# Causal attention: the mask of the diagonal blocks is added by VectorE instead of by a product with the identity

## The reference

```
h = _layernorm(x, ln_w, ln_b)
h = conv over time, 3 taps, one filter for each channel
q, k, v = split(h @ attn_w)            # 16 heads of 8 channels, rotary positions on q and k
scores = q @ k^T / sqrt(8)
scores = where(causal, scores, -1e30)
y = softmax(scores) @ v
x = x + y @ proj_w
```

## Time and profile before

| what | value |
|---|---|
| median of 3 runs | 1771.7 us (1768.62 to 1781.09) |
| profiled execution | 1771.55 us, span of its records 1769.7 us |
| TensorE busy, all of the span | 1417.7 us (80%) |
| VectorE busy | 1041.1 us (59%) |
| ScalarE busy | 704.1 us (40%) |
| GpSimd busy | 572.9 us (32%) |
| L998, reductions of the rounds of L0f | 88, 97.2 us in all |
| L904, mask products of L0f | 176, one pair a round |
| first and last reduction of L998 | 293.3 and 468.0 us from the start |

### The profile page before, as it was taken

The page is one execution under the profiler, slowest core; times in us unless marked ns, Lnnn a source line. Parts: engine busy times, 40 slices in busy tenths (PEclk is TensorE's granted clock), DMA queues, the critical chain, the costliest instruction groups (busy, mean ns, idle before and its releaser), DMA issues. The chain is left out here.

```text
span 1769.7 us, 23757 instructions
## 1 busy us (share of the span) xinstructions
PE 1417.7 (80%) x8978; PEld 724.7 (41%) x8980; DVE 1041.1 (59%) x1468; ACT 704.1 (40%) x1306; POOL 572.9 (32%) x594
## 2 busy tenths in 40 slices
PE   5868755788858999699668986699999657689984
PEld 3345522333333444344234434354554232256553
DVE  3698736677642222578366752466676145468866
ACT  2444431666720000277334753244444221255522
POOL 1477713453302110332113301634422100047660
PEclk7789986899969999889886996899999669879986
DMA  3000010000010000100010002000000000000000
GB/s 102 0 1 0 1 44 1 1 1 1 1 75 0 0 0 0 50 1 1 9 49 1 1 1 44 1 1 1 2 2 1 1 29 0 6 1 1 2 1 26
DMA packets 19154, 20.58 MB, mean 12 GB/s; under 512 B 9803, under 2 KB 15163, under 8 KB 18408
## 3 DMA queue, kind: packets, MB, share of 16 engines
q1 hardware_dynamic: 18024, 19.07, 3.5%
q10 hardware_dynamic: 1024, 0.07, 0.0%
HBM read 17.94 MB, written 1.05 MB: 11 GB/s over the span
## 5 line engine op out<-in xcount | busy, mean ns | idle before, releaser
L1663 ACT ACTIVATE L2f_prob<-P 128x512 f32<-128x512 f32 x160 | 86.8, 595 | 112.6 <-PE P L1601 112.6
L998 DVE TENSOR_REDUCE L0f_nm<-P 128x2 f32<-128x768 f32 (+3 forms) x88 | 97.2, 1121 | 42.7 <-PE P L904 42.5
L2174 PE MATMUL P<-L0m_hm,L0m_w 128*128 128x512 f32 x256 | 112.5, 600 | 2.6 <-POOL L0m_hm L2136 2.6
L1691 DVE TENSOR_REDUCE L2f_nm<-P 128x2 f32<-128x768 f32 (+3 forms) x88 | 99.2, 1128 | 3.0
L1601 PE MATMUL P<-L2f_qs,L2f_ks 49*128 49x384 f32 (+3 forms) x512 | 94.3, 477 | 7.7 <-ACT L2f_prob L1663 3.9
L954 ACT ACTIVATE L0f_prob<-P 128x512 f32<-128x512 f32 x160 | 87.3, 601 | 29.4 <-PE P L917 26.9
L1517 POOL TENSOR_SCALAR_AFFINE_SELECT L2f_prob<-L2f_prob 128x512 f32<-128x512 f32 x64 | 39.7, 635 | 168.1 <-ACT L2f_prob L1663 168.0
L1690 DVE TENSOR_TENSOR P<-P,L2f_mask 128x256 f32<-128x256 f32 (+2 forms) x88 | 48.4, 550 | 74.3 <-PE P L1587 73.1
L1587 PE MATMUL P<-L2f_ks,L2f_qs 48*128 48x384 f32 (+3 forms) x512 | 87.7, 451 | 3.4 <-DVE L2f_nm L1691 3.4
L2516 POOL TENSOR_TENSOR L3x_exm<-L3x_exm,L3x_rec 128x2048 f32<-128x2048 f32 x16 | 72.3, 4526 | 26.1 <-DVE L3x_rec L2690 26.1
L2174 PEld LDWEIGHTS P<-L0m_hm,L0m_w 128*128 128x128 f32 x256 | 49.2, 193 | 64.9 <-issue 62.8
(11 more groups left out here) (575 smaller groups left out, 3298.7 us busy)
## 6 DMA issues: line engine op xcount, KB each, us to landing
L0m_w<-in_L0m_w SPq DMA_DIRECT2D x1, 2048.0 KB, 7.7
L0f_va<-in_L0f_va SPq DMA_DIRECT2D x3, 512.0 KB, 4.7
in_xt<-in_x SPq DMA_DIRECT2D x1, 1024.0 KB
L0x_segi<-in_segb SPq DMA_DIRECT2D x1, 1024.0 KB, 5.0
L0m_w<-in_L0m_w SPq DMA_DIRECT2D x1, 1024.0 KB, 9.7
out<-out_o SPq DMA_DIRECT2D x4, 256.0 KB, 2.5
L1x_va<-in_va SPq DMA_DIRECT2D x3, 256.0 KB, 3.1
L1x_vr<-in_vr SPq DMA_DIRECT2D x3, 256.0 KB, 4.3
```

The source lines that it names most:

```text
L998: nc.vector.tensor_reduce(S.nm[:, qt, first:first + 2 * many].rearrange("p (i e) -> p e i", e=2), P[:, bank:bank + 2, 0:many * width].rear ...
L1663: nc.scalar.activation(S.group_prob(b, g)[:, slot, :], P[:, bank, :], ACT.Exp).then_inc(*S.act_done.up())
L1691: nc.vector.tensor_reduce(S.nm[:, qt, first:first + 2 * many].rearrange("p (i e) -> p e i", e=2), P[:, bank:bank + 2, 0:many * width].rear ...
L2174: m = mm(P[:, bank, :], lhs, hm[:, e, :], start=e == 0, stop=e == E - 1)
```

## The change

TensorE no longer multiplies the identity with the mask. In each round the products of L901 are now complete by themselves, and the last of them signals s_full. VectorE, when the round is full, adds the mask to the diagonal blocks of both banks in PSUM with one instruction (in place), waits for its end, and reduces as before. The order of the steps is the same.

```diff
                     for p in range(many):
                         for e in range(2):
                             pair = 4 * half + many * i + p
-                            mm(P[:, bank + e, p * width:(p + 1) * width], S.qs1[b % 2][64 * e:64 * e + 48, pair, qt * 128:(qt + 1) * 128],
-                               S.ks[b % 2][64 * e:64 * e + 48, pair, 0:width], start=p == 0, stop=False)
-                    for e in range(2):
-                        m = mm(P[:, bank + e, 0:many * width].rearrange("p (h k) -> p h k", k=width)[:, :, width - 128:width],
-                               G["identb"][:], mask[:].unsqueeze(1).to_broadcast([128, many, 128]), start=False, stop=True)
+                            m = mm(P[:, bank + e, p * width:(p + 1) * width], S.qs1[b % 2][64 * e:64 * e + 48, pair, qt * 128:(qt + 1) * 128],
+                                   S.ks[b % 2][64 * e:64 * e + 48, pair, 0:width], start=True, stop=True)
                     m.then_inc(*S.s_full.up())
...
                     first = 8 * half + 2 * many * i
+                    diag = P[:, bank:bank + 2, 0:many * width].rearrange("p e (i k) -> p e i k", k=width)[:, :, :, width - 128:width]
+                    over = mask[:].unsqueeze(1).unsqueeze(1).to_broadcast([128, 2, many, 128])
+                    link(dve, nc.vector.tensor_tensor(diag, diag, over, ALU.add), S.vstep)
                     nc.vector.tensor_reduce(S.nm[:, qt, first:first + 2 * many].rearrange("p (i e) -> p e i", e=2),
```

## The result

| | before | changed |
|---|---|---|
| median, 6 runs each | 1771.53 us (1768.62 to 1781.09) | 1793.68 us (1791.96 to 1796.29) |
| profiled execution | 1771.55 us, span 1769.7 | 1792.71 us, span 1791.0 |

The changed kernel is slower by 22 us: the ratio is 1.0115, with a 95% interval of 1.0087 to 1.0142.

What follows compares the result with a forecast made beforehand. VectorE was taken to bound the lead and to end each stretch's chain, with no engine full in the stretches. Lead 5.7, stretches 14.5 and clock 3.0 made 23.2 us on 1771.55: 1795 us, range 1784 to 1807.

Steps and rivals of the forecast that it cites:

- What bounds it: Phase L0f: VectorE bounds the lead; in seven stretches no engine is full, each a chain ending through VectorE.
- Price of the additions: VectorE in L0f: each addition costs 1.27, 0.72 or 0.46 us by width, 51.1 us for eight halves.
- Lead, +5.7: L0f's opening, only first-half rounds: VectorE never idle, so additions fully paid, 6.39 less 0.69 us for removed products.
- Stretches, lag 12.5 to 16.0, taken 14.5: L0f's seven steady stretches: added VectorE time carried as a lag that waits shrink, 12.5 to 16.0 us, taken 14.5.
- one of the prediction's own signs of being wrong: Splitting of the maxima before the transposes: forecast wrong if its 1.85 us became shorter or longer.
- Clock, +3.0, two of five blocks turned slow: Transpose blocks after each split: longer TensorE standing turns two of five fast blocks half-speed, 1.5 us each, +3.0.
- After the last maximum nothing moves: L0f's last pass, without rounds, and everything behind it: only the start shifts, no added time.
- Later phases: Phases behind L0f, which the change doesn't touch: counted at nothing.
- The one within 1%: Lead and stretches: VectorE packs its work and head waits close, 13.3 us, 1785; chance 0.15 for within 1%.
- The third, clock and feedback at +33: L0f: all five blocks turn slow and later bank pairs hold up exponentials, 33.2 us, 1805; chance 0.25.

Runs made afterwards that it cites:

- e1: Changed kernel without its 88 additions, so no mask at all in the L0f rounds; 1771.95 us, ratio 1.0012 to the kernel before.
- e2: Kernel before with the 88 VectorE additions put in and TensorE's mask products kept, so the mask is added twice; 1792.81 us, ratio 1.0114.
- e7: Changed kernel with every mask addition made twice; 1830.55 us in one run, 36.9 us over the changed kernel.
- e3: Changed kernel with six unneeded TensorE products ahead of its wait for the split maxima, once a half; 1792.72 us, ratio 1.0117.
- e9: Changed kernel with three unneeded TensorE products ahead of each exponential step of the last pass only; 1800.3 us (2 runs).
- e11: Kernel before with VectorE additions replacing mask products only in the lead's eleven rounds; 1775.91 us, ratio 1.0021.
- e4: Kernel before with six unneeded TensorE products ahead of its wait for the split maxima, once a half; 1771.71 us, ratio 0.9988.
- e10: Kernel before with VectorE additions replacing mask products only in the last two halves' rounds; 1775.06 us, ratio 1.0020.

## Why the prediction was right, point by point

The time was 1793.7 for a forecast of 1795, the sign and the size were right. By its own terms:

**What bounds it** held. TensorE's products were worth nothing (e1 in the total, e2 in the stretches), although TensorE had the highest busy time. VectorE became the bound (157.08 of 172.56 us, e7 97%).

**Price of the additions** held: 1.26, 0.73 and 0.47 us from start to start in the timeline above and its neighbours, against 1.27, 0.72 and 0.46 in L2f. VectorE's busy time in all rose by 41.1 us and not by about 48: the 88 additions by themselves sum to 47.8, but the split of the maxima became 3.8 us shorter over its eight times, and more of VectorE's instructions overlap.

**Lead, +5.7:** measured 5.3 (changed, e2, e3, e9 and e11, all at 26.3). The products that I took off, 0.69, are not in it, and can't be: this length starts with VectorE's first round, behind the first pair of products. Ahead of it VectorE waited 11.15 us before and 10.64 in the changed kernel, so the pair was worth about 0.5. What is in the 5.3 is a shorter split of the maxima, 1.6 us from the start of L418 to the block in place of 2.6.

**Stretches, lag 12.5 to 16.0, taken 14.5:** measured 11.75 (e3 less e4, with some of the clock left in it), below the range of this term. The order by stretch is right in the middle (1.9, 2.5, 1.8, 2.2 for 1.7, 2.6, 1.6, 2.7), and too large in the first, the sixth and the last (-0.3, 0.2, 3.5 for 0.8, 2.1, 4.5). The count took the split as fixed, and its change was one of the prediction's own signs of being wrong. From the start of the split to the block it was 1.8 us before the block at 453.48, and it is 1.15 before that at 469.39:

```profile
469.39 1.38 PE L372 MATMUL P<-identb,L0f_qk 128*128 128x128 bf16 x16 [2.24 <-DVE L0f_qk L421]
```

with L418 starting at 468.24, in the row of the timeline above. The four small instructions ran beside GpSimd's clearing of the exponentials (L867), and where they now begin, it is done. The traces of all kernels bear this out (last section): with no GpSimd instruction beside them the four took 1.09 to 1.11 us in each of 31 splits. In e10, where only the last two stretches changed, only the last two splits became as short.

**Clock, +3.0, two of five blocks turned slow:** measured 3.4 (changed less e3; an estimate, since e3 still has three slow blocks and the filler takes time itself), but by another count: three of the five turned fully slow and the other two in part (1.40 and 1.38 us), and in the mean each cost less than my 1.5.

**After the last maximum nothing moves:** wrong. The last pass took 5.0 us more, by the clock. I had looked for the clock's effect only at the block behind each wait, and the eighth block, the one at the head of the last pass, I priced like the rest. But there TensorE went on at half speed for 17 us. Its short stands between the exponentials don't explain that: they are 0.78 us in the kernel before as well, where the clock held (second line of each pair: before).

```profile
499.98 0.61 PE L914 MATMUL P<-L0f_qs,L0f_ks 51*128 51x384 bf16 x4 [0.78 <-ACT L0f_prob L951]
476.66 0.40 PE L917 MATMUL P<-L0f_qs,L0f_ks 51*128 51x384 bf16 x4 [0.78 <-ACT L0f_prob L954]
503.34 0.61 PE L914 MATMUL P<-L0f_qs,L0f_ks 51*128 51x512 bf16 x2 [0.78 <-ACT L0f_prob L951]
479.01 0.39 PE L917 MATMUL P<-L0f_qs,L0f_ks 51*128 51x512 bf16 x2 [0.78 <-ACT L0f_prob L954]
```

Over all kernels without filler in it the length of this pass ("last" in the table) goes with the clock granted in it: 21.9 us at 0.93, 23.0 at 0.89, 23.2 at 0.87, 23.7 at 0.86, 24.0 at 0.82, 25.7 at 0.77, and 26.8 to 26.9 at 0.69. What sets the clock there stays open. This term was mis-sized from 0 to 5.0.

**Later phases** I left at nothing, and they gave back 4.1 us, for which I find no cause in the change. Without the later phases and the last pass, the terms as measured give nearly the same: 5.3 + 11.75 + 3.4 = 20.45 us, 1792.0. The 5.0 and the 4.1 nearly cancel by chance, so the agreement to 1.3 us is better than the working deserves; on the two profiled executions it is 21.2 us against 23.2.

**Rivals.** The one within 1% priced packed work at 13.3 us, 7.5 of it in the stretches. The head waits did close in part (31.4 to 10.1 us), and the measured lag of 11.75 lies between its 7.5 and my 14.5, just under the 12.0 that I had named as the border; the clock decided against it. The third, clock and feedback at +33, put the clock at 7.5; it was 3.4 in the stretches and 5.0 behind them. Its feedback is not separated by any run: TensorE's waits for the bank pairs did rise (17.1 us of its weight loads, 1.7 before), and ScalarE's waits for the exponentials' products rose from 26.7 to 36.0 us in the seven stretches. A lag below the count leaves little room for it, no more.

## What to carry to other kernels

Price a moved operation by the waits of the engine that gets it, in the order in which they lie, not by its share of busy time: the same kind of instruction cost 3 us in all where waits follow it, and 21 where they don't, of which 16 to 17 in the stretches and the lead. An engine that reads as the busiest may give nothing when it is spared, and it may even lose clock: look also at the stretches that the edit leaves alone, and don't put down what you see there to the edit before the same has shown in a second and third variant. And when total times of edits differ by less than the later phases move by themselves, cut the trace at one recurring point and compare lengths.

## What the runs showed of the hardware that I had not expected

TensorE's clock fell to 0.69 over a whole pass of unchanged instructions after edits ahead of it (21.9 us before, 26.8 in e1 and 26.9 in the changed kernel). Which edits do it follows no rule that I found: in e10 the products of the last two stretches are gone too and it was 0.87, and with all products of the stretches in place it was 0.93, 0.86 and 0.82 (before, e2, e11). TensorE's short stands in this pass were the same 0.78 us at either clock. The Trainium skill (TensorE: Matmul & The Clock Gate, "What's actually happening") says that half speed is the default and that activity releases it; e9 agrees, 0.85 with more work in the same place, at no gain in time, but no run here shows what made the same work hold the clock in one kernel and not in the other.

The four instructions that split the maxima took 1.1 to 3.5 us in one and the same kernel, the changed one. The Trainium skill (SBUF — State Buffer, "Who interferes with whom") says that a VectorE instruction with two SBUF inputs contends with a GpSimd instruction that reads SBUF. The rows fit it: the subtraction L419, whose two inputs lie in SBUF, took 0.21 us in the timeline behind 468 us and 1.17 us at 369.23, where GpSimd was at work on the next sequence's splitting. Over the 104 splits in the 13 traces it took 0.21 or 0.22 us in all 48 with no GpSimd instruction beside it, 0.51 to 0.53 beside the clearing L867 alone (17 times), and 0.28 to 1.18 beside other work of GpSimd (39 times). The casts, with one input, became slower too: L420 took 0.24 or 0.25 us alone and up to 1.23 beside GpSimd.

```profile
369.23 1.17 DVE L419 TENSOR_TENSOR L0f_nmr<-L0f_nm,L0f_qk 128x32 f32<-128x32 f32 x1
...
468.51 0.21 DVE L419 TENSOR_TENSOR L0f_nmr<-L0f_nm,L0f_qk 128x32 f32<-128x32 f32 x1
```
